# One row chunk at a time from ScalarE in the first tile, and the last two states summed bank by bank

## The reference, cut to what matters

```python
x = layernorm(x + L0(x, adj))
x = layernorm(x + L1(x, adj))

# L0, N = 4096 nodes, D = 128 features: two stacks on the same adjacency
ax = adj @ x1                       # x1 = x for stack 1, another input x2 for stack 2
h = ax + (1 + eps) * ax
for i in range(3): h = relu(h @ W[i].T + b[i])
out = concat(h_stack1, h_stack2) @ Wm.T + bm

# L1: h = layernorm(relu(adj @ x @ gcn_w + gcn_b)), then a Mamba block
xc, z = split(h @ w_in)             # 256 inner channels
u = silu(causal_conv4(xc) + conv_b)
dt, B, C = parts of u @ w_xp        # dt through w_dt and softplus
state[d, s] = exp(dt*A)[d, s] * state[d, s] + dt*B*u      # 16 states s
y = sum over s of state[d, s] * C[s]  + u * D_skip
out = (y * silu(z)) @ w_out
```

## Time and profile before

| | us |
|---|---|
| median of 3 runs | 1115.28 |
| lowest, highest | 1114.30, 1115.93 |
| the profiled execution, its own time | 1119.08 |
| its span, first to last instruction | 1117.5 |
| busy in it: PE, DVE | 992.0 (89%), 1026.8 (92%) |
| busy in it: ACT, POOL | 547.8 (49%), 278.6 (25%) |
| HBM traffic | 226 MB, 202 GB/s over the span |

### The profile page before, as it was taken

How to read it: one execution, slowest core, us unless ns; L and a number is a source line. 1 busy time by engine, 2 the same in 40 slices (tenths; PEclk the granted TensorE clock), 3 DMA queues, 4 the chain that set the end, 5 groups by cost and what they waited for, 6 DMA issues and landing times. The chain is left out here.

```text
span 1117.5 us, 13236 instructions
## 1 busy us (share of the span) xinstructions
PE 992.0 (89%) x4162; PEld 688.9 (62%) x4162; DVE 1026.8 (92%) x782; ACT 547.8 (49%) x1065; POOL 278.6 (25%) x200
## 2 busy tenths in 40 slices
PE   2879999999999999999998989989989899876665
PEld 1667777777777777534555646646656556554554
DVE  5979999999999999744999999999999999999995
ACT  3342443444344343416464575755756658447451
POOL 5430202020202020201322324323333243232331
PEclk9899999999999999999998999989989999887676
DMA  9999999999999999975634345255352461101000
GB/s 245 255 239 296 335 309 348 320 354 324 333 335 335 343 326 342 161 251 205 220 104 152 132 170 175 76 191 183 101 185 111 169 225 57 57 19 46 32 19 19
DMA packets 190535, 226.33 MB, mean 203 GB/s; under 512 B 8640, under 2 KB 164352, under 8 KB 176160
## 3 DMA queue, kind: packets, MB, share of 16 engines
q1 hardware_dynamic: 105936, 163.60, 45.5%
q10 hardware_dynamic: 81040, 53.23, 18.6%
q0 software_dynamic: 3520, 9.04, 2.9%
HBM read 162.66 MB, written 63.18 MB: 202 GB/s over the span
## 5 line engine op out<-in xcount | busy, mean ns | idle before, releaser
L855 DVE STREAM_TRANSPOSE at<-rows 128x1024 f32<-128x1024 f32 x136 | 267.8, 2011 | 26.4 <-DMA adjT<-at 9.6
L1083 PE MATMUL yT<-ah,xh 128*128 128x512 f32 x512 | 213.9, 418 | 37.3 <-DVE al L863 29.4
L522 POOL TENSOR_TENSOR dBuP<-dtu,b_sb 128x1024 f32<-128x1024 f32 x64 | 152.1, 2377 | 361.5 <-DVE hs L1022 181.5
L562 ACT ACTIVATE ah<-at 128x2048 fp32r<-128x2048 f32 x64 | 122.6, 1915 | 213.8 <-PE yT L1083 198.2
L1170 PE MATMUL bank<-adjc,xm 128*128 128x512 f32 x448 | 207.6, 598 | 0.8 <-ACT axT L643 0.8
L1083 PE MATMUL yT<-al,xh 128*128 128x512 f32 x512 | 203.2, 397 | 0.0
L1083 PE MATMUL yT<-ah,xl 128*128 128x512 f32 x512 | 202.8, 396 | 0.0
L738 ACT ACTIVATE dA<-dt,A_sb 128x512 f32<-128x512 f32 x256 | 169.4, 711 | 54.6 <-DVE dt L968 54.6
L1255 PE MATMUL yT<-ident,pr 128*128 128x128 f32 x1024 | 158.2, 308 | 35.1 <-DVE pr L1029 35.1
L1255 PEld LDWEIGHTS yT<-ident,pr 128*128 128x128 f32 x1024 | 138.4, 160 | 64.9 <-DVE pr L1029 50.5
L1022 DVE TENSOR_TENSOR_SCAN hs<-dA,zero,dBuP 128x1026 f32<-128x1026 f32 x64 | 158.4, 2476 | 0.0
(11 more groups left out here) (165 smaller groups left out, 989.0 us busy)
## 6 DMA issues: line engine op xcount, KB each, us to landing
adjT<-at SPq DMA_DIRECT2D x56, 1024.0 KB, 7.7
adjc<-adjT SPq DMA_DIRECT2D x56, 1024.0 KB, 4.8
rows<-in_adj SPq DMA_DIRECT2D x152, 256.0 KB, 8.5
rows<-in_adj ACTq DMA_DIRECT2D x136, 256.0 KB, 8.9
b_sb<-b_dram ACTq DMA_DIRECT2D x32, 512.0 KB, 3.8
xm<-in_x SPq DMA_DIRECT2D x4, 512.0 KB, 11.7
res<-in_x POOLq DMA_DIRECT2D x8, 256.0 KB, 8.1
mid<-xn POOLq DMA_DIRECT2D x8, 256.0 KB, 7.7
```

Of the source, the lines that this page charges most:

```text
L522: nc.gpsimd.tensor_tensor(dBu(n, par)[:, :, 1:], dtu[par][:, :, :], b_sb[pair % 2][:, nB(n) % 2:nB(n) % 2 + 1, :].to_broadcast([P, H, TILE ...
L562: nc.scalar.activation(ah[c % 2][:, :], at[c % 2][:, :, :].rearrange("p m t -> p (m t)"), ACT.Copy)\
L855: last = nc.vector.transpose(dst.rearrange("p m (g i) -> p g m i", i=32), src.rearrange("p g (i m) -> p g m i", i=32))
L1083: last = mm(acc[k][:, :], w[:, b, :], v[c % 2][:, cols], start=(b == 0 and j == 0), stop=(b == KB - 1 and j == 2))
```

## The change

In the first tile ScalarE issued chunks 2, 3 and 4 behind copy 0, and from then on chunk c + 4 behind copy c and the x copies of that pass. Now a table says what each pass issues: chunk 2 in pass 0, 3 and 4 in pass 1, 5, 6 and 7 in passes 2, 3 and 4, 8 and 9 in pass 5, 10 and 11 in passes 6 and 7. Later tiles are as before. At the end, the sums of the last tile's states 14 and 15 run over bank 0 first and then over bank 1, each with both channel halves, and a new semaphore `last_summed` counts after each bank of state 15, so that each half of `last_gate` waits for its own bank. The number of instructions on each engine is the same.

```diff
--- before.py
+++ after.py
@@ -44,6 +44,7 @@
 CONV = (0, 0, 0, 0, 0, 0, 0, 4, 4, 0, 0, 0, 0, 0, 0, 0)
 PLAN = (2, 4, 1, 2, 3, 3, 3, 0, 0, 0, 0, 2, 3, 3, 3, 3)
 AHEAD = sum(PLAN[AT['pe_gcn']:])
+FIRST_ROWS = ((2,), (3, 4), (5,), (6,), (7,), (8, 9), (10,), (11,))
 C_IN_O = (0, 2, 4, 6)
 POOL = (1, 3, 5, 7, 9, 11, 13, 15)
 POOL_AFTER = 3
@@ -243,6 +244,7 @@
         skip_ready, y_turned, y_ready = sem("skip_ready"), sem("y_turned"), sem("y_ready")
 
         y_gated, projected = sem("y_gated"), sem("projected")
+        last_summed = sem("last_summed")
         last_gated, last_projected = sem("last_gated"), sem("last_projected")
 
         o_mean, o_squares, o_var_eps, o_inv_dev = sem("o_mean"), sem("o_squares"), sem("o_var_eps"), sem("o_inv_dev")
@@ -584,13 +586,14 @@
             def stage_a(it, mlp, norm):
                 for c in range(CHUNKS):
                     hi(it, c)
-                    if not mlp and c == 0:
-                        load_rows(act, (2, 3), 0, 2)
-                        load_rows(act, (2, 3), 0, 3)
                     if not mlp and c in (1, 2, 4):
                         x_hi(c // 2 + 1)
-                    after = it + (c + NROWS) // CHUNKS
-                    load_rows(act, (2, 3), 0 if isinstance(after, int) and after == TILES else after, (c + NROWS) % CHUNKS)
+                    if mlp:
+                        after = it + (c + NROWS) // CHUNKS
+                        load_rows(act, (2, 3), 0 if isinstance(after, int) and after == TILES else after, (c + NROWS) % CHUNKS)
+                    else:
+                        for m in FIRST_ROWS[c]:
+                            load_rows(act, (2, 3), m // CHUNKS, m % CHUNKS)
                     if mlp and c == 0:
                         first(it - 1)
                     if mlp and c in (2, 4, 6):
@@ -977,9 +980,9 @@
                                         sz[par][:, :, :].rearrange("p q d -> p (q d)"), ALU.mult).then_inc(y_gated, 1)
 
             def last_gate():
-                dve.wait_ge(summed, S * TILES)
                 dve.wait_ge(gate_ready, 2 * TILES)
                 for j in range(2):
+                    dve.wait_ge(last_summed, j + 1)
                     nc.vector.tensor_tensor(yg[:, 2 * j:2 * j + 2, :].rearrange("p q d -> p (q d)"), yT[:, TILE * j:TILE * j + TILE],
                                             sz[1][:, 2 * j:2 * j + 2, :].rearrange("p q d -> p (q d)"), ALU.mult)\
                         .then_inc(last_gated, 1)
@@ -1369,7 +1372,16 @@
             window(6, 0, True, True, False)
             window(7, 1, True, False, False)
             for k in LATE:
-                sum_state(TILES - 1, k)
+                pe.wait_ge(C_multiplied, S * (TILES - 1) + k + 1)
+                for j in range(2):
+                    for h in range(H):
+                        for q in range(2 * j, 2 * j + 2):
+                            last = mm(yT[:, DI * q + P * h:DI * q + P * h + P], pr[k % NPR][:, h, P * q:P * q + P], ident[:, :],
+                                      is_transpose=True, start=False, stop=k == S - 1 and h == 1 and q % 2 == 1)
+                    if k == S - 1:
+                        last.then_inc(last_summed, 1)
+                if k < S - 1:
+                    last.then_inc(summed, 1)
             pe.wait_ge(o_normed, RG * (TILES - 1))
             pe.wait_ge(C_multiplied, S * TILES)
             pe.wait_ge(x1_tile_in[1], 8 * (TILES - 2) + 16)
```

## The result

| | before | after |
|---|---|---|
| median, us | 1115.93 | 1124.99 |
| lowest, highest | 1114.30, 1118.57 | 1123.70, 1126.38 |
| runs | 5 | 5 |
| the profiled execution, its span | 1119.08, 1117.5 | 1124.29, 1122.7 |

The changed kernel takes 1.0077 times as long (95% interval 1.0058 to 1.0096), which of 1115.93 is 8.6 us more (the two medians differ by 9.1), where 1.7 were forecast and the range ended 4.4 above the median. The profiled executions differ by 5.2 us only. The comparison of runs is the measure, the traces show where.

What follows compares the result with a forecast made beforehand. After 84 us TensorE and VectorE are tight, so what counts is how far that stretch's start moves. Part 1 +1.7 and part 2 0 took the profiled 1119.08 to 1120.8, 1117.0 us on the median's scale; range 1112.5 to 1119.7.

Steps and rivals of the forecast that it cites:

- The gain: First tile: copy 1 starts when chunk 1 is turned, at 21.25, and everything hanging on it is 2.7 us earlier.
- that gives 31.5: just in time: Chunk 3's second half, issued at about 22, lands in 9.5 us; its turn, wanted at 31.6, does not wait.
- 12 and not 9.5: Rival: chunk 3's second half needs 12 us, its turn waits 2.4 us; +1.7 + 2.4, 1119.4 us; chance 0.08.
- The issue of chunk 7: Pass 4, behind the copies of x part 3: its loads go out at 52.4 and 52.8, 14 us later than before.
- I take 62.7, nearer to the quiet pair: Chunk 7's second half lands at 62.7, nearer to a 9.5 us pair issued at 69 us with only rows in flight.
- the old pair: Row loads issued at this point of the old kernel, among the weights; the second half landed 11.6 us after issue.
- My rival with 11.6 us: Rival: chunk 7 lands like the pair among the weights, at its turn; +3.4, 1118.7 us; chance 0.23.
- rule on completion across queues: Completion follows every earlier write of the same DMA engine; chunk 7 would wait for GpSimd's weight loads: +3.4 instead of +1.7.
- X - 61.0: Shift of chunk 6's end for chunk 7 landing at X, if TensorE starts slowly after idling: 62.3 and 64.4 give +1.3, +3.4.
- X - 62.5: The same shift of chunk 6's end without a fall of TensorE's clock: 62.3 and 64.4 give -0.2 and +1.9.
- The queue: Pass 5 on ScalarE: the six-load burst puts copy 6 at about 62.3, done 64.2, hidden before it is wanted at 66.7.
- Part 2 at 0: Last two states bank by bank: first gate 0.8 us earlier, transposes unmoved, so 0; bounds 0.8 gain, 0.1 loss.

Runs made afterwards that it cites:

- in-place kernels: Chunks 2, 3 in pass 0, 4, 5 in pass 1, rest as in the kernel before: 0.9991; x2 part 3 early too: 0.9971; plus new tail 0.9963, or early weights 0.9955.
- the one with only chunk 7 put back: New row-load table with old tail, but chunks 5 and 6 in pass 2, chunk 7 back in pass 3: 1.0012 of the kernel before.
- rows-only kernel: Kernel before with only the new table of row loads, tail as before: 1124.79 us, 1.0057 of the kernel before.
- only chunk 7 late: Row loads as in the kernel before, except chunk 7 issued in pass 4 behind the copies of x part 3, with chunk 8: 1.0045 of the kernel before.
- x2 part 2 early: Full new table, old tail, GpSimd issuing x2 part 2 right behind part 1, about 13 us instead of 21: 1.0052 of the kernel before.
- the kernel with the weights early: Full new table, old tail, GpSimd's last 11 weight loads issued when chunk 2 is turned instead of behind x2 part 3: 1.0022 of the kernel before.
- the kernel with chunk 7 ahead of x part 3: Full new table, old tail, chunk 7 issued in pass 4 ahead of the two copies of x part 3 instead of behind: 1.0028 of the kernel before.

## Why the prediction was wrong, step by step

**The gain: right.** Copy 1 at 20.72 (about 21.3 forecast), the hole before the subtraction 1.98 us (2 forecast). The turn of chunk 2 at 27.15 (27.65 forecast). Some 0.4 us of the lead in the trace is an earlier first chunk (turned at 7.97, before at 8.35) and not the change. The in-place kernels show that the lead is carried on if nothing eats it.

**Chunk 3: wrong.** The step was "that gives 31.5: just in time", from a 9.5 us landing of a row with little ahead of it in its own queue. The second half took 12.9 us and the turn waited 3.50. I had that as a rival, "12 and not 9.5", with a chance of 0.08. It is what happened in each of the six kernels with the full new table, and in the one with only chunk 7 put back: waits from 2.6 to 6.1 us. The row chosen was of another queue, 9 us earlier in the kernel; the load of chunk 3 stood still beside SP's rows and then shared the engines with x2 part 2.

**The issue of chunk 7: nearly right.** 52.4 and 52.8 forecast, 53.46 and about 53.8 measured. That is luck in part, two errors that nearly cancel: the wait at chunk 3 had GpSimd issue x2 part 3 at 49.3 and not at 46.4, 2.9 us later than forecast, and the faster x2 load (4.1 us, not 6.0) gave 1.9 back.

**The landing of chunk 7: the step that failed.** "I take 62.7, nearer to the quiet pair", 9.9 us after the issue. It was 13.3 in the changed kernel, and 11.5, 11.7 and 10.8 in the three others with chunk 7 as late and the weights in place (the rows alone, only chunk 7 late, x2 part 2 early). I argued from ScalarE's own queue (fewer loads ahead, empty for a while). The experiments show that this was the wrong thing to count. With the weight loads gone the same pair takes 4.5 us; issued just before them, 5.9; as they begin, 7.7; in their midst, 10.8 to 13.3. What these runs show is that the landing goes by what is in flight from the other queues at and after the issue. The trace of before could have told it: from 55.14, the issue of the old pair, to 59.0 us ScalarE's queue moved no packet, and the others moved 0.83 MB. How it divides between the weights and SP's rows is not shown. My rival with 11.6 us had the right neighbours, but took too little even so. The range ended at 1119.7 because I let that rival (1118.7) and the one on chunk 3 (1119.4) be alternatives. Both came true: the landing added 3.4 us, and chunk 3, less the quick x2 load, 1.0 to the issue.

The Trainium skill, "DMA: Bandwidth & Descriptors", section "Queues, rings and completion order", says that each DMA engine goes round the queues that have work, a packet at a time. The trace of before agrees in a stretch where all three queues have work, 27 to 28 us:

```profile
q0 software_dynamic: 64, 0.26, 80.0%
q1 hardware_dynamic: 63, 0.03, 13.0%
q10 hardware_dynamic: 62, 0.03, 12.8%
```

Equal packets, and GpSimd's hold eight times the bytes of the others'. The rule does not say why a queue with loads issued moves nothing for 4.7 us. The same section's rule on completion across queues, which I had quoted against my own choice, pointed to the slow case too. No run here tells its part from that of the shared engines: moving the weights takes away both. From 58.5 to 64 us ScalarE's queue moved 0.56 MB, about the size of the pair, and the pair landed at 67.1; whether the 3 us between are such a wait, the trace does not show.

**From the late turn to the end of chunk 6: right.** By "X - 61.0" a landing at 67.1 gives +6.1; measured +6.3. The slower level of TensorE's clock came as forecast: the granted clock is 0.50 from 72 to 76 us, which is 1.2 of 2.4 GHz. The trace of after, TensorE's products of chunk 6 (the first two, the tenth and the last):

```profile
73.21 0.80 PE L1086 MATMUL yT<-ah,xh 128*128 128x512 f32 x1 [7.88 <-DVE al L866]
73.80 0.63 PE L1086 MATMUL yT<-ah,xl 128*128 128x512 f32 x1
...
77.06 0.39 PE L1086 MATMUL yT<-ah,xh 128*128 128x512 f32 x1
...
80.25 0.40 PE L1086 MATMUL yT<-al,xh 128*128 128x512 f32 x1
```

After 7.88 us of idle time the first products take 0.63 us each, those from 77.06 on 0.39; the chunk takes 7.4 us from its first start to its last end. Before, all of it took 5.5 us at clock 1.00. In the rows-only kernel and the one with x2 part 2 early the formula is 1.0 to 1.1 us short (X = 66.23 gives +5.2, measured +6.3), and 1.3 too much where only chunk 7 is late. There the clock did not fall in chunk 6, and it is the other formula that holds: X - 62.5 gives +3.8 for 66.33, measured +4.0. So the two formulas are good to about 1 us, if one knows how long TensorE stands idle first.

**The queue: half right.** The burst held ScalarE 3 us longer than forecast (65.4, not 62.3) and still hid behind the late turn, by 1.65 us.

**Part 2 at 0: right.** The gate moves by 0.8 us as forecast, the transposes behind it by nothing, and the kernel with that part alone measures 1.0001, within 0.23%.

**The scale: a smaller error.** I subtracted the 3.8 us by which before's profiled execution lay above the median. The other groups of runs put its median at 1117.5 to 1118.5, so that execution was an ordinary one. The kernel before spreads by up to 8.3 us from run to run, the changed one by 2.7. In the first comparison before ran low (1115.93), which adds some 2 us to the difference: the rows-only kernel is +6.3 us against 32 runs of before, the changed kernel, 0.2 us from it in its median, +8.6 against 5. The two intervals overlap from 1.0058 to 1.0079. In the traces the miss is 4.6 us (6.3 for 1.7), and 4.4 of it is that chunk 7 is there at 67.1 instead of 62.7: 3.4 from the time to landing, 1.0 from the issue.

**What stays open.** What makes the kernel before spread; what the weights and what SP's rows each do to chunk 7's 13.3 us and to chunk 3's 12.9; why ScalarE's queue stands still for 4.7 us behind an issue in one kernel and for 1 in another; the rest of the 3 us by which the kernel with chunk 7 ahead of x part 3 lies above before.

## What to carry to other kernels

When a load is moved later, price its landing by all that is in flight on the shared DMA engines at its new issue time, from every queue; how empty its own queue is says little (here 4.5 us with little beside it, and 13.3 beside weights and SP's rows). Move only the loads that block: taking chunk 4's held pair out of the burst kept the gain, while issuing chunk 7's pair 15 us later cost more than the gain was worth. Two late loads on one chain add up (in the traces 1.0 us with chunk 3 late, 4.0 with chunk 7, 6.3 with both, the excess no more than the slower clock cost), so their rivals belong in one case and not in two.

## What the runs showed of the hardware that was not expected

A load that has been issued can stand still while other queues move, with nothing ahead of it in its own. In the trace of after this was so for 4.7 us at chunk 7, and for 2.5 us at chunk 3, once its queue had run dry at 24.3 us (the rows and numbers above). In the kernel with the weights early it was about 1 us.

The same kind of row load moves at very unlike rates while the engines are shown as busy. The trace of after from 24.5 to 26.5 us, when only SP's rows move (ScalarE's are issued and stand still), and from 30.5 to 34 us, when both queues move, with 0.49 and 0.48 MB; then the kernel with the weights early from 59.3 to 60 us, when only ScalarE's rows move (packets, MB, mean rate):

```profile
DMA packets 706, 0.36 MB, mean 182 GB/s; under 512 B 20, under 2 KB 698, under 8 KB 706
...
DMA packets 1992, 0.99 MB, mean 282 GB/s; under 512 B 106, under 2 KB 1984, under 8 KB 1992
...
DMA packets 427, 0.21 MB, mean 305 GB/s; under 512 B 10, under 2 KB 427, under 8 KB 427
```

The first two suggest that two queues with equal loads are faster than one, by half. The third, one queue at 305 GB/s for 0.7 us, shows that it isn't so simple. The Trainium skill, "DMA: Bandwidth & Descriptors", section "Issuing engines are not separate DMA queues", says that issuing from several engines saves only the sequencer's time; these stretches neither bear it out nor refute it, since what sets the rate of a single queue stays open.

From 27 to 28 us of before, GpSimd's queue moved 0.26 MB in 64 packets and ScalarE's 0.03 in 62 (the rows above): where the queues take turns, the one with large packets gets several times the bytes, and rows, cut into small ones, get what is left. The same 256 KB load landed in 13.3 us in one kernel and in 4.5 in another, where it was issued 4.3 us later, after the weights and nearly all of SP's rows.
